# Self and cross attention: key product and probability transposes ahead of the output, query and value products

## The reference

```python
x = _layernorm(x + _L0_attn_ref(x, L0_attn_w_qkv, L0_attn_w_proj, L0_attn_b_proj), axis=-1)
x = _layernorm(x + _L0_xattn_ref(x, ctx_1024, ctx_1024, ...), axis=-1)
x = _layernorm(x + _L0_ffn_ref(x, ...), axis=-1)
...
```

## Time and profile before

| | us |
|---|---|
| median of 3 runs | 1884.66 |
| lowest and highest run | 1882.13, 1884.88 |
| the profiled execution, time | 1890.28 |
| the profiled execution, span in the profile | 1888.5 |
| self attention, its constant stretch | 29.40 to 170.99 |
| cross attention, its constant stretch | 221.51 to 374.25 |
| TensorE, matmul busy over the span | 1654.7 (88%) |
| VectorE busy | 1165.1 (62%) |
| ScalarE busy | 906.1 (48%) |
| GpSimd busy | 639.2 (34%) |

### The profile page before, as it was taken

How to read it: one execution, slowest core, us unless ns; L and a number is a source line. 1 busy time by engine, 2 the same in 40 slices (tenths; PEclk the granted TensorE clock), 3 DMA queues, 4 the chain that set the end, 5 groups by cost and what they waited for, 6 DMA issues and landing times. The chain is left out here.

```text
span 1888.5 us, 51651 instructions
## 1 busy us (share of the span) xinstructions
PE 1654.7 (88%) x18030; PEld 1361.0 (72%) x18030; DVE 1165.1 (62%) x3270; ACT 906.1 (48%) x2607; POOL 639.2 (34%) x966
## 2 busy tenths in 40 slices
PE   6998599958799999999999996799999999997660
PEld 4776477748677777777777775798888988896450
DVE  4776367647466766767776765456666666665106
ACT  3665266624245544544444452455555555553220
POOL 2555255411023333333323332233333333332016
PEclk9999799969899999999999999899999999999885
DMA  1111411102101001010010010311111111111354
GB/s 47 42 38 34 153 49 49 48 20 59 36 20 33 23 27 28 22 31 25 22 33 23 24 32 12 92 55 46 47 52 54 54 45 48 51 55 36 106 141 82
DMA packets 169607, 89.32 MB, mean 47 GB/s; under 512 B 17665, under 2 KB 166450, under 8 KB 169138
## 3 DMA queue, kind: packets, MB, share of 16 engines
q1 hardware_dynamic: 162402, 77.35, 14.7%
q10 hardware_dynamic: 5072, 6.66, 1.0%
q0 software_dynamic: 2048, 4.20, 1.0%
HBM read 65.07 MB, written 23.07 MB: 47 GB/s over the span
## 5 line engine op out<-in xcount | busy, mean ns | idle before, releaser
L1121 PE MATMUL bank<-diff_xT,diff_w_score 128*128 128x128 f32 x2048 | 259.8, 281 | 0.8 <-ACT diff_xT L1225 0.8
L1121 PEld LDWEIGHTS bank<-diff_xT,diff_w_score 128*128 128x128 f32 x2048 | 242.4, 193 | 22.4 <-issue 20.6
L1232 ACT ACTIVATE diff_keys<-bank 128x512 f32<-128x512 f32 x256 | 152.7, 597 | 166.1 <-PE bank L1121 166.1
L1866 POOL TENSOR_TENSOR lat_prob<-lat_prob,lat_inv_sum 128x512 f32<-128x512 f32 x128 | 133.4, 1042 | 228.3 <-DVE lat_inv_sum L1797 227.4
L1415 POOL TENSOR_TENSOR diff_prob<-diff_prob,diff_inv_sum 128x512 f32<-128x512 f32 x64 | 67.1, 1049 | 380.5 <-DVE diff_inv_sum L1319 380.5
L1699 ACT ACTIVATE lat_prob<-bank,lat_neg_max 128x128 f32<-128x128 f32 x512 | 181.5, 372 | 11.4 <-DVE lat_neg_max L1815 11.3
L1710 ACT ACTIVATE lat_query<-bank 128x512 f32<-128x512 f32 x128 | 76.6, 598 | 181.6 <-PE bank L1595 181.6
L1625 PE MATMUL bank<-lat_catT,lat_query 128*128 128x128 f32 x1024 | 142.5, 283 | 3.9 <-ACT lat_query L1710 3.9
L1595 PE MATMUL bank<-lat_catT,lat_w_score 128*128 128x128 f32 x1024 | 138.1, 279 | 1.4 <-DVE lat_mask_bias L1843 1.0
L1605 PE MATMUL bank<-lat_probT,lat_c_rep 32*128 32x256 f32 x2048 | 131.2, 393 | 6.0 <-DVE lat_z L1802 5.6
L1625 PEld LDWEIGHTS bank<-lat_catT,lat_query 128*128 128x128 f32 x1024 | 126.0, 194 | 8.1 <-ACT lat_query L1710 5.4
(11 more groups left out here) (302 smaller groups left out, 3596.7 us busy)
## 6 DMA issues: line engine op xcount, KB each, us to landing
lat_c_rep<-cat SPq DMA_DIRECT2D x128, 128.0 KB, 2.7
diff_x_rep<-stage SPq DMA_DIRECT2D x128, 32.0 KB
lat_c_t<-cat SPq DMA_DIRECT2D x32, 128.0 KB, 2.2
exp_w<-in_L_ffn_w_dram SPq DMA_DIRECT2D x16, 256.0 KB
self_x_t<-in_x_dram SPq DMA_DIRECT2D x32, 64.0 KB
self_x_res<-in_x_dram SPq DMA_DIRECT2D x32, 64.0 KB
stage<-self_y SPq DMA_DIRECT2D x32, 64.0 KB
cross_x_t<-stage SPq DMA_DIRECT2D x32, 64.0 KB
```

What stands on the lines that cost most here:

```text
L1121: last = nc.tensor.matmul(ring[(k + d) % 2][:, j * P:(j + 1) * P], w_score[:, H1 * (k // 2) + HS * d + 4 * (k % 2) + j, :], xT[:, :], star ...
L1232: nc.scalar.activation(keys[:, k // 2, 4 * (k % 2):4 * (k % 2) + 4, :].rearrange("p h t -> p (h t)"), ring[(k + d) % 2][:, :], ACT.Copy).t ...
L1866: nc.gpsimd.tensor_tensor(prob[:, q, :, :], prob[:, q, :, :], inv_sum[:, q, :, None].to_broadcast([P, 4, T]), ALU.mult)\
```

## The change

The products go in another order on TensorE: k, then the eight transposes of the probabilities, then the output product, then q, then v, then AV. The values are written to the bank `ps_t[0]`, which also takes the first half of the transposed probabilities, instead of the bank of q and k. For that the semaphore `qkv_done` is split in three, and waits are added: the transposes wait until the values of the slot before have been copied (`v_ready`), q waits for the copy of kT, v waits for the first probability copy. On ScalarE the copy of qT goes behind the two probability copies, and the copy of v goes between the two exponentials; it still waits for AV of its slot. xT of the next slot stays behind all of them.

```diff
--- before.py
+++ after.py
@@ -187,9 +187,9 @@
         rstd = sb("rstd", [P, 2, 1])
         y = sb("y", [P, 2, P])
 
-        ps_qkv, ps_tail = core.bank[0], core.bank[1]
+        ps_qk, ps_tail = core.bank[0], core.bank[1]
         ps_t = [core.bank[2], core.bank[3]]
-        ps_x = ps_t[1]
+        ps_v, ps_x = ps_t[0], ps_t[1]
         ps_s = [core.bank[4 + g] for g in range(4)]
         ps_o = ps_tail[:, 0:VW * H0 // 2].rearrange("p (g e) -> p g e", e=VW)
         ps_oT, ps_out = ps_tail[:, 2 * P:3 * P], ps_tail[:, 3 * P:4 * P]
@@ -198,7 +198,8 @@
         res_loaded = [sem(f"res_loaded{p}") for p in range(2)]
         stored = [sem(f"stored{p}") for p in range(2)]
         xt_done, xT_ready = sem("xt_done"), sem("xT_ready")
-        qkv_done, qT_ready, kT_ready, v_ready = sem("qkv_done"), sem("qT_ready"), sem("kT_ready"), sem("v_ready")
+        k_done, q_done, v_done = sem("k_done"), sem("q_done"), sem("v_done")
+        qT_ready, kT_ready, v_ready = sem("qT_ready"), sem("kT_ready"), sem("v_ready")
         kd_ready = sem("kd_ready")
         s_done, max_done, sub_done, exp_done = sem("s_done"), sem("max_done"), sem("sub_done"), sem("exp_done")
         inv_done, ones_done = sem("inv_done"), sem("ones_done")
@@ -295,32 +296,36 @@
                 if here(on, i, 1):
 
                     wait(pe, xT_ready, i + 2)
-                    wait(pe, v_ready, i + 1)
+                    wait(pe, qT_ready, i + 1)
                     kv = xT[:, 1 if cross else 0, :]
-                    nc.tensor.matmul(ps_qkv[:, 0:P], wq[:, :], xT[:, 0, :], start=True, stop=True)
-                    nc.tensor.matmul(ps_qkv[:, P:2 * P], wk[:, :], kv, start=True, stop=True)
-
-                    for b in range(2):
-                        for odd in range(2):
-                            last = nc.tensor.matmul(ps_qkv[odd * S:(odd + 1) * S, (2 + b) * P:(3 + b) * P],
-                                                    kv[:, b * S:(b + 1) * S], wv[:, odd, :], start=True, stop=True)
-                    last.then_inc(qkv_done, 1)
-                if here(on, i, -2):
-
-                    wait(pe, oT_ready, i - 1)
-                    nc.tensor.matmul(ps_out, oT[:, :], wo[:, :], start=True, stop=True).then_inc(out_done, 1)
+                    nc.tensor.matmul(ps_qk[:, P:2 * P], wk[:, :], kv, start=True, stop=True).then_inc(k_done, 1)
                 if here(on, i, -1):
 
+                    wait(pe, v_ready, min(i + 1, NPAIR) if isinstance(i, int) else i + 1)
                     for c in range(2):
                         wait(pe, exp_done, 2 * i - 1 + c)
-                        wait(pe, pT_ready, 2 * i - 3 + c)
                         for hp in range(4):
                             src = prob[:, 1 - par, 8 * c + 2 * hp:8 * c + 2 * hp + 2, :].rearrange("p h t -> p (h t)")
                             last = nc.tensor.transpose(ps_t[c][:, hp * P:(hp + 1) * P], src, core.ident[:, :])
                         last.then_inc(t_done, 1)
+                if here(on, i, -2):
+
+                    wait(pe, oT_ready, i - 1)
+                    nc.tensor.matmul(ps_out, oT[:, :], wo[:, :], start=True, stop=True).then_inc(out_done, 1)
+                if here(on, i, 1):
+
+                    wait(pe, kT_ready, i + 2)
+                    nc.tensor.matmul(ps_qk[:, 0:P], wq[:, :], xT[:, 0, :], start=True, stop=True).then_inc(q_done, 1)
+
+                    wait(pe, pT_ready, 2 * i - 1)
+                    for b in range(2):
+                        for odd in range(2):
+                            last = nc.tensor.matmul(ps_v[odd * S:(odd + 1) * S, b * P:(b + 1) * P],
+                                                    kv[:, b * S:(b + 1) * S], wv[:, odd, :], start=True, stop=True)
+                    last.then_inc(v_done, 1)
+                if here(on, i, -1):
 
                     wait(pe, z_done, i - 1)
-                    wait(pe, v_ready, i)
                     for hp in range(8):
                         if hp % 4 == 0:
                             wait(pe, pT_ready, 2 * i - 1 + hp // 4)
@@ -334,11 +339,17 @@
 
         @block.scalar
         def _(act):
+            def exps(i, par, c):
+
+                wait(act, sub_done, 2 * i + 1 + c)
+                half = prob[:, par, 8 * c:8 * c + 8, :].rearrange("p h t -> p (h t)")
+                nc.scalar.activation(half, half, ACT.Exp).then_inc(exp_done, 1)
+
             def slot(i, k, par, on):
                 if here(on, i, 1):
 
                     wait(act, xt_done, i + 2)
-                    wait(act, qkv_done, i + 1)
+                    wait(act, v_done, i + 1)
                     n = 2 if cross else 1
                     nc.scalar.activation(xT[:, 0:n, :].rearrange("p m t -> p (m t)"), ps_x[:, 0:n * P], ACT.Copy)\
                         .then_inc(xT_ready, 1)
@@ -349,11 +360,9 @@
                     nc.scalar.activation(oT[:, :], ps_oT, ACT.Copy).then_inc(oT_ready, 1)
                 if here(on, i, 1):
 
-                    wait(act, qkv_done, i + 2)
+                    wait(act, k_done, i + 2)
                     wait(act, s_done, 2 * i)
-                    nc.scalar.activation(kT[:, 1 - par, :], ps_qkv[:, P:2 * P], ACT.Copy).then_inc(kT_ready, 1)
-                    nc.scalar.activation(qT[:, 1 - par, :], ps_qkv[:, 0:P], ACT.Copy, scale=float(HD0) ** -0.5)\
-                        .then_inc(qT_ready, 1)
+                    nc.scalar.activation(kT[:, 1 - par, :], ps_qk[:, P:2 * P], ACT.Copy).then_inc(kT_ready, 1)
                 if here(on, i, -1):
 
                     wait(act, av_done, i - 1)
@@ -361,18 +370,22 @@
                         wait(act, t_done, 2 * i - 1 + c)
                         nc.scalar.activation(probT[:, 4 * c:4 * c + 4, :].rearrange("p h e -> p (h e)"), ps_t[c][:, :],
                                              ACT.Copy).then_inc(pT_ready, 1)
+                if here(on, i, 1):
+
+                    wait(act, q_done, i + 2)
+                    nc.scalar.activation(qT[:, 1 - par, :], ps_qk[:, 0:P], ACT.Copy, scale=float(HD0) ** -0.5)\
+                        .then_inc(qT_ready, 1)
                 if here(on, i, 0):
-
-                    for c in range(2):
-                        wait(act, sub_done, 2 * i + 1 + c)
-                        half = prob[:, par, 8 * c:8 * c + 8, :].rearrange("p h t -> p (h t)")
-                        nc.scalar.activation(half, half, ACT.Exp).then_inc(exp_done, 1)
+                    exps(i, par, 0)
                 if here(on, i, 1):
 
+                    wait(act, v_done, i + 2)
                     wait(act, av_done, i)
                     nc.scalar.activation(v_blk[:, 1 - par, :, :, 0:2 * HD0],
-                                         ps_qkv[:, 2 * P:4 * P].rearrange("p (b g e) -> p b g e", b=2, e=2 * HD0),
+                                         ps_v[:, 0:2 * P].rearrange("p (b g e) -> p b g e", b=2, e=2 * HD0),
                                          ACT.Copy).then_inc(v_ready, 1)
+                if here(on, i, 0):
+                    exps(i, par, 1)
 
             for weights in early:
                 weights.start(act)
```

## The result

| | median, us | lowest to highest | ratio to before, 95% interval |
|---|---|---|---|
| before | 1883.39 | 1880.89 to 1884.88 | |
| changed | 1839.41 | 1834.22 to 1840.98 | 0.9758 (0.9738 to 0.9778) |
| changed, again in a later comparison (before there: 1886.09) | 1839.79 | 1837.89 to 1841.09 | 0.9763 (0.9746 to 0.9780) |

A forecast was written before the change was run, and what follows sets the result against it. TensorE's order, with AV waiting for ScalarE's probability copy, was taken to bound the attention slots. Saving 0.37 in self and 0.66 in cross over 29 slots each gives 29.9 us: 1884.7 to 1854.8, say 1855, range 1849 to 1869.

The forecast's parts named there:

- step (b): ScalarE's chain v_blk, exp c1, xT delays k to 1.39 in self, 1.49 to 1.50 in cross; stall 0.34 and 0.06.
- step (e): Sum over 29 slots a phase: 29.9 us saved; filling and draining slots 0, with 2 us either way.
- What bounds the kernel: TensorE's order sets the beat; AV's wait for ScalarE's probability copy is the large one, about 0.35 us a slot between matmuls.
- Step (a): TensorE's new order: copies run under out, q and v; k's load to next slot 3.27, v to AV 0.46.
- TensorE alone would be ready at 1.05: Start of k in a self slot if TensorE did not wait for xT: 1.05 us into the slot.
- the sign that I gave: Profile after: TensorE idle ahead of k about 0.3 us a self slot, released by ScalarE's xT; almost none in cross.
- Step (c): Bill per slot: self 4.66 against 5.03, 0.37 less; cross 4.76 against 5.42, 0.66 less.
- Step (d): Late next: scores covered by 0.1 to 0.2, exp c1 covered, cross input loads keep at least 3.2 us.
- Rival 1: AV must wait for v's end, or ScalarE's chain is 0.05 to 0.1 slower; saving 18.6, 1866 us; chance 0.12.
- Rival 2: The stall only moves: chain AV, v_blk, exp c1, xT, k 0.5 us longer per slot; 1881 to 1888; chance 0.05.
- Rival 3: Granted clock falls to 1.2 GHz at the pause ahead of k in self; slower, 1902 us; chance 0.04.
- Rival 4: More than forecast: lower bounds of the slot's steps, saving 32; 1852.5, or 1850.5 with phase ends; chance 0.03.

The follow-up runs named there:

- q_last: The changed kernel with q between v and AV on TensorE (order k, transposes, out, v, q, AV); 1864.08 us, ratio 0.9878.
- q_early: The changed kernel with q right behind k again (order k, q, transposes, out, v, AV); 1846.78 us, ratio 0.9796.
- pT_wait_first: The kernel before with AV's wait for the first probability copy ahead of its waits for z and v_blk; 1882.12 us, ratio 0.9985.
- x_first: The changed kernel with exp c1 moved on ScalarE behind xT of the next slot; 1834.97 us, ratio 0.9735.
- both warm: The kernel before and the changed kernel, each with dummy matmuls where TensorE waits in self and cross; 1881.80 and 1838.75 us.

## Why the prediction was right or wrong

The direction and the mechanism held, the size did not: 44 us against 30, 1839.4 where the range ended at 1849. About half of the missing 14 us is in the constant slots, where step (b) had the hand-off from xT to TensorE too long (0.12 instead of 0.05), and half at the ends of the phases, which step (e) put at 0 (6.9 and 9.4 us in two profiles).

- **What bounds the kernel.** Right. AV's wait for the copy was the large one, and it is gone.
- **Step (a), TensorE's order.** Right to a few hundredths: from k's load to the next slot 3.27 forecast, 3.22 to 3.25 measured. The choice for v to AV was between 0.44, with no wait for v's end, and 0.59; the rows show 0.38, then 1.13 for AV instead of 1.07, 1.51 in all against 1.53. q_last shows what the other order would have cost. q as cover for the copy (0.06 thin) was right too: q_early lost 0.15 without it, where 0.08 to 0.16 was expected.
- **Step (b), the new chain through ScalarE.** v_blk, exp c1 and xT stand at 0.18, 0.46 and 0.98, where 0.20, 0.46 and 0.98 were forecast. The last term was mis-sized: 0.12 from xT to TensorE, read off AV's row, is 0.05, and xT lasts 0.27 instead of 0.29. k starts at 1.30 instead of 1.39 in self, and in cross at 1.44 instead of 1.49, where TensorE's own 1.43 decides. pT_wait_first explains the row I had taken: AV stood behind two further waits. The trace of the kernel before held a row with 0.05, the output transpose behind the normalised output, and I did not compare. "TensorE alone would be ready at 1.05" was wrong. In the shorter slot VectorE's stats end 0.29 into the next one, the reciprocal starts at 0.32 instead of 0.18, and the output transpose at 1.03. That alone would hold k until 1.20. It cost nothing in this kernel, since 1.30 was later. But it makes the sign that I gave wrong: TensorE's wait in self is the one ahead of the output transpose, released by VectorE, and xT holds k for only 0.10 of the 0.25 by which k starts later than 1.05.
- **Step (c), the bill per slot.** 0.37 and 0.66 forecast, 0.53 and 0.77 measured. Of the missing 0.16 in self, 0.09 are the start of k, up to 0.05 what follows it, and the rest the 0.03 by which the mean of the slots before lay over the one slot that was read; in the changed kernel, with slots of 4.51 and 4.55, it does not. In cross 0.05 and 0.05 are the same two. Over 28 slots of each phase that is 7.7 us. (The stretch that the prediction calls 3rd to 31st transpose is the 4th to the 32nd; the number of slots, 28 and one more, is right.)
- **Step (d), what is late next.** Scores and exp c1 were covered, as said, and no load was waited for. The one chain that I did not follow, stats to reciprocal to output transpose to k, is the one that is next in line; x_first ran into it.
- **Step (e), the ends at 0, with 2 us either way.** This term failed by as much as the slots: 9.4 us in the first profile and 6.9 in the second. The slots that fill and empty also hold the pair copy and AV, or k and its copy, and gained by the same order: both warm, self filling is 1.1 us shorter; with the clock up in both, self emptying is 1.0 shorter, 0.5 of it the last full slot. The other part is the clock, which I had weighed only as a danger, and it is partly luck. In the profile of before it fell at 177.9, in the emptying of self (its last 32 AV matmuls take 1.90 us), in those of the changed kernel only behind AV; that is 2.4 us, and other runs show the fall with either order. In the emptying of cross, 2.6 us shorter, 0.8 is the last full slot and about 1.5 again the clock: the last transposes and AV take 1.90 and 1.79 us before, and 1.04 and 1.11 at the upper clock. How the gain in the fillings divides is shown for self alone.
- **The rivals.** Rival 1 (v's end must be waited for) fell: no drain between v and AV. Rival 2 (the stall only moves) fell; a stall did move, k starts 0.25 us later in self, but that is less than the 0.71 (0.58 and 0.13, the terms of step (c)) that the new order frees. Rival 3 (the clock falls at k) fell: 1.00 in both stretches. Rival 4 was closest, with the wrong term: not the lower bounds inside the slot but the hand-off and the ends.

The range was too narrow because its lower end kept the hand-off of 0.12, read off a single row, as if it had no lower bound, and gave the ends 2 us without working them out from a slot of the filling or emptying stretch, although the trace had them.

## What to carry to other kernels

When a matmul waits for a copy, put the products that depend on nothing new between the transposes and the matmul, and choose among them one of the same tile form to stand last; here 0.45 us a slot hung on q standing before v instead of behind it (0.10 of it a wait for the copy). After removing a wait, follow every chain that closes in the shorter slot, not only the one through the moved instructions, and cost the first and last slots as slots of their own. Take a hand-off between engines from several rows, and two profiles for any stretch in which the clock changes: here the emptying of self took 20 us in the changed kernel and 22 in two close variants of it, and the clock made the difference. Where several waits stand ahead of one matmul, try putting the one that will end last first; here that was worth 0.06 us a slot.

## What the runs showed of the hardware

- A wait that ends last releases TensorE in 0.05 us when it stands first of the waits ahead of a matmul, and in 0.12 when it stands last of three: 0.06 us a slot in both phases.
- Matmuls of one form flow into each other: AV's first weights load 0.38 us after v's, while v, 0.66 us long, still runs. Two changes of form more in a slot cost 0.3 us.
- Pauses of 0.3 to 0.55 us between TensorE's loads in each slot of 4.5 to 5.5 us left the granted clock at 1.00 in all stretches of constant slots. It fell at the ends of the phases, in some executions before the last AV and in others behind it, whatever the order; the fall is worth 2.4 us. With dummy matmuls in the first slot it was up from 13.5 us on instead of 27.8 (by the durations), worth 4 us of the whole time in the kernel before and nothing measurable in the changed one.
